# Mamba slots of a two-layer mixer: C products and u merged on GpSimd, neighbouring B products merged, the residual added by TensorE and copied by ScalarE, and the four engines' orders rewritten

## What is computed

```python
def _mamba_block(x, in_w, cw, cb, xp_w, dt_w, dt_b, A_log, D_skip, out_w):
    xm, z = jnp.split(jnp.einsum('bld,ed->ble', x, in_w), 2, axis=-1)
    ...                                   # causal convolution over 4 taps
    xm = jax.nn.silu(jnp.transpose(xc, (0, 2, 1)) + cb[None, None, :])
    dt, Bm, Cm = jnp.split(jnp.einsum('bld,ed->ble', xm, xp_w), [DT_RANK, DT_RANK + D_STATE], axis=-1)
    dt = jax.nn.softplus(jnp.einsum('blr,dr->bld', dt, dt_w) + dt_b)
    dA = jnp.exp(dt[..., None] * -jnp.exp(A_log))
    dBu = dt[..., None] * Bm[:, :, None, :] * xm[..., None]
    _, h = jax.lax.associative_scan(_scan_combine, (dA, dBu), axis=1)
    y = jnp.einsum('blds,bls->bld', h, Cm) + xm * D_skip
    return jnp.einsum('bld,od->blo', y * jax.nn.silu(z), out_w)

for i in range(N_LAYERS):
    x = x + _mamba_block(_layer_norm(x, ln_g, ln_b), ...)
```

## Time and profile before

| | us |
|---|---|
| median of 3 runs | 1511.6 (1506.72, 1511.6, 1511.95) |
| the profiled execution, its own time | 1509.6 |
| its span, first to last instruction | 1506.9 |
| PE busy in the span | 1297.4 (86%) |
| DVE busy | 1170.8 (78%) |
| POOL busy | 1129.8 (75%) |
| ACT busy | 1003.6 (67%) |

### The profile page before, as it was taken

One profiled execution on the slowest core, in us unless ns is written; L12 is line 12 of the kernel. 1 busy time (PEld: TensorE's weight loads), 2 busy tenths in 40 slices (PEclk: granted clock), 3 DMA queues, 4 the chain that ended last, 5 costly groups with the idle time before them and its releaser, 6 DMA issues.

```text
span 1506.9 us, 20348 instructions
## 1 busy us (share of the span) xinstructions
PE 1297.4 (86%) x5459; PEld 718.6 (48%) x5460; DVE 1170.8 (78%) x1739; ACT 1003.6 (67%) x2373; POOL 1129.8 (75%) x775
## 2 busy tenths in 40 slices
PE   5589988998999899989988899799489889888984
PEld 2233333333333333333433567799455556555653
DVE  7599999999999999999999866655344555455554
ACT  3587778777877887787778872333266666666673
POOL 6499999999999999999999950344456556554551
PEclk8799999999999999999999999899799999999996
DMA  4543363255335433642452514311200000000000
GB/s 162 226 169 127 154 244 152 102 202 210 127 130 231 169 138 142 243 162 103 191 225 114 181 61 140 98 49 47 67 14 8 13 16 22 12 10 9 8 9 7
DMA packets 49122, 169.33 MB, mean 112 GB/s; under 512 B 15720, under 2 KB 33580, under 8 KB 40860
## 3 DMA queue, kind: packets, MB, share of 16 engines
q1 hardware_dynamic: 46780, 163.84, 28.7%
q0 software_dynamic: 2272, 4.66, 1.3%
HBM read 160.81 MB, written 7.67 MB: 112 GB/s over the span
## 4 chain that ended last, share of the span: by engine, by line
PE 31%; DVE 25%; issue 16%; ACT 13%; POOL 13%; DMA 1%; DVEq 0%; POOLq 0%; ACTq 0%
DVE h L1226 12%; POOL h L1232 9%; DVE h L1205 6%; ACT banks L1189 6%; PE banks L399 5%; PE banks L723 3%; PE banks L782 3%; PE banks L761 2%; PE banks L408 2%; POOL h L1212 2%; PE banks L797 2%; PE banks L700 2%; PE banks L663 2%; PE banks L680 2%; ACT Cb L740 1%
## 5 line engine op out<-in xcount | busy, mean ns | idle before, releaser
L1232 POOL TENSOR_TENSOR h<-h,Cb 128x1024 f32<-128x1024 f32 x255 | 595.5, 2356 | 31.8 <-DVE h L1226 30.5
L1226 DVE TENSOR_TENSOR_SCAN h<-banks,h 128x1024 f32<-128x1024 f32 x256 | 575.7, 2279 | 16.3 <-ACT banks L1189 12.4
L1259 PE MATMUL banks<-h,ident 128*128 128x512 f32 x1024 | 481.3, 603 | 49.0 <-POOL h L1232 26.9
L1189 ACT ACTIVATE banks<-dt,A_cur 128x255 f32<-128x255 f32 x1024 | 424.8, 462 | 136.8 <-DVE h L1226 134.8
L1259 PEld LDWEIGHTS banks<-h,ident 128*128 128x128 f32 x1024 | 185.6, 190 | 310.3 <-issue 207.5
L1205 DVE TENSOR_TENSOR h<-Bb,banks 128x1024 f32<-128x1024 f32 x176 | 210.5, 1204 | 0.0
L1212 POOL TENSOR_TENSOR h<-Bb,u 128x1024 f32<-128x1024 f32 x80 | 189.0, 2363 | 0.6 <-POOL u L1158 0.6
L753 POOL TENSOR_SCALAR h<-h 128x128 f32<-128x128 f32 (+1 forms) x128 | 101.4, 807 | 106.5 <-DVE h L746 106.5
L753 POOL TENSOR_SCALAR Cb<-Cb,h 128x128 f32<-128x128 f32 (+1 forms) x128 | 96.0, 766 | 53.7 <-DVE h L746 53.6
L1087 PE MATMUL banks<-xn,wF 128*128 128x512 f32 x256 | 119.0, 609 | 10.2 <-ACT xn L1079 10.2
L770 DVE COPY Bb<-banks 128x384 f32<-128x384 f32 x64 | 35.5, 555 | 75.5 <-PE banks L761 72.7
(11 more groups left out here) (289 smaller groups left out, 2042.3 us busy)
## 6 DMA issues: line engine op xcount, KB each, us to landing
Bb<-scrX SPq DMA_DIRECT2D x32, 2048.0 KB, 7.1
Cb<-scrX SPq DMA_DIRECT2D x32, 2048.0 KB, 11.3
h<-in_L_ffn_w SPq DMA_DIRECT2D x2, 2048.0 KB, 8.4
by_expert<-Cb SPq DMA_DIRECT2D x39, 64.0 KB, 1.5
h<-in_conv_w SPq DMA_DIRECT2D x4, 512.0 KB, 3.9
scr<-h SPq DMA_DIRECT2D x3, 640.0 KB, 3.0
wF<-scr SPq DMA_DIRECT2D x3, 512.0 KB
dt<-in_pmask SPq DMA_DIRECT2D x4, 257.0 KB, 2.8
```

Source lines behind the costliest of these rows:

```text
L1189: m = e.activation(ps_dA[c % 2][:, g, half, 1:S], dts[q][:, half, i * S + 1:(i + 1) * S], ACT.Exp, scale=A_cur[q][:, s:s + 1])
L1226: e.tensor_tensor_scan(chunk(i, c), ps_dA_flat[c % 2], chunk(i, c), 0.0, ALU.mult, ALU.add).then_inc(sem("scan"), 1)
L1232: e.tensor_tensor(h[i][:, rows(c), :, :], h[i][:, rows(c), :, :], both(Cb[i], c), ALU.mult).then_inc(sem("hC"), 1)
L1259: m = e.matmul(bank(5), ident[:], h_flat[i][:, s * HALVES * S:(s + 1) * HALVES * S], start=(s == 0), stop=(s == NS - 1))
```

## The change

1. **POOL.** `pool_C` and `pool_mul` take several neighbouring chunks, and one instruction then covers them all; it raises its semaphore by the number of chunks when the last is done, and `pool_C` waits for the last chunk's scan. In slots 0 to 14 six pairs of C products become one instruction each (a0 a1, a2 a3, a5 a6, b0 b1, b3 b4, b5 b6). The two halves of u become one instruction of 128 x 1024.
2. **DVE.** The B products a1 a2, b1 b2 and b4 b5 become one instruction each, and DVE's products move ahead of the scans: in the new list no product stands directly before the scan of its own chunk.
3. **Residual.** `pe_out` adds one identity matmul over `xs` ahead of the two output matmuls, all into bank 5, so that PE adds the residual. ACT (`act_res`) copies bank 5 into `xs`; DVE no longer takes part, but for the very last pair.
4. **Orders.** All four lists of slots 0 to 14 are rewritten. The last slot keeps the unmerged order on POOL (`POOL_LAST`) and loses `res` on DVE, gains it on ACT.

The diff, cut where a list has only lines that stay as they are:

```diff
--- before.py
+++ after.py
@@ -1151,21 +1151,25 @@
             e.scalar_tensor_tensor(out=dts[q][:], in0=ps_dt, scalar=0.0, in1=sp[:], op0=ALU.max, op1=ALU.add
                                    ).then_inc(sem("dt"), 1)
 
-        def product_u(e, t, q, half):
+        def product_u(e, t, q, *half):
             e.wait_ge(sem("dt"), t + 1)
-            e.wait_ge(sem("xm"), 2 * t + half + 1)
+            e.wait_ge(sem("xm"), 2 * t + (half[0] + 1 if half else HALVES))
             wait(e, sem("ub"), 2 * t - 2)
-            e.tensor_tensor(us[q][:, half, :], dts[q][:, half, :], xm[q][:, half, :], ALU.mult
-                            ).then_inc(sem("u"), 1)
-        def rows(c):
-            return slice(GROUP * c, GROUP * c + GROUP)
-
-        def both(t, c):
-            return t[:, rows(c), :].unsqueeze(2).to_broadcast([P, GROUP, HALVES, S])
+            at = slice(half[0], half[0] + 1) if half else slice(0, HALVES)
+            e.tensor_tensor(us[q][:, at, :], dts[q][:, at, :], xm[q][:, at, :], ALU.mult
+                            ).then_inc(sem("u"), 1 if half else HALVES)
+        def rows(cs):
+            return slice(GROUP * cs[0], GROUP * cs[-1] + GROUP)
+
+        def both(t, cs):
+            return t[:, rows(cs), :].unsqueeze(2).to_broadcast([P, GROUP * len(cs), HALVES, S])
+
+        def u_rows(t, cs):
+            return t.unsqueeze(1).to_broadcast([P, GROUP * len(cs), HALVES, S])
 
         def act_ucopy(e, p, q, i):
             e.wait_ge(sem("u"), 2 * p + 2)
@@ -1198,20 +1202,18 @@
                 if i:
                     e.wait_ge(sem("scr"), 16 * (LAYERS - 1))
 
-        def dve_mul(e, p, q, i, c):
-            if c == DVE_MUL[i][0]:
+        def dve_mul(e, p, q, i, *cs):
+            if cs[0] == DVE_MUL[i][0]:
                 e.wait_ge(sem("ub"), 2 * p + i + 1)
             mul_ready(e, p, i)
-            e.tensor_tensor(h[i][:, rows(c), :, :], both(Bb[i], c),
-                            ps_u.unsqueeze(1).to_broadcast([P, GROUP, HALVES, S]), ALU.mult
-                            ).then_inc(sem("mulv"), 1)
-
-        def pool_mul(e, p, q, i, c):
+            e.tensor_tensor(h[i][:, rows(cs), :, :], both(Bb[i], cs), u_rows(ps_u, cs), ALU.mult
+                            ).then_inc(sem("mulv"), len(cs))
+
+        def pool_mul(e, p, q, i, *cs):
             e.wait_ge(sem("u"), 2 * p + 2)
             mul_ready(e, p, i)
-            e.tensor_tensor(h[i][:, rows(c), :, :], both(Bb[i], c),
-                            us[q][:, :, i * S:(i + 1) * S].unsqueeze(1).to_broadcast([P, GROUP, HALVES, S]), ALU.mult
-                            ).then_inc(sem("mulp"), 1)
+            e.tensor_tensor(h[i][:, rows(cs), :, :], both(Bb[i], cs), u_rows(us[q][:, :, i * S:(i + 1) * S], cs), ALU.mult
+                            ).then_inc(sem("mulp"), len(cs))
 
         def chunk(i, c):
             n = GROUP * HALVES * S
@@ -1226,16 +1228,16 @@
             e.tensor_tensor_scan(chunk(i, c), ps_dA_flat[c % 2], chunk(i, c), 0.0, ALU.mult, ALU.add
                                  ).then_inc(sem("scan"), 1)
 
-        def pool_C(e, p, q, i, c):
-            e.wait_ge(sem("scan"), CHUNKS * (2 * p + i) + c + 1)
+        def pool_C(e, p, q, i, *cs):
+            e.wait_ge(sem("scan"), CHUNKS * (2 * p + i) + cs[-1] + 1)
             e.wait_ge(sem(f"C{i}"), 16 * p + 16)
-            e.tensor_tensor(h[i][:, rows(c), :, :], h[i][:, rows(c), :, :], both(Cb[i], c), ALU.mult
-                            ).then_inc(sem("hC"), 1)
+            e.tensor_tensor(h[i][:, rows(cs), :, :], h[i][:, rows(cs), :, :], both(Cb[i], cs), ALU.mult
+                            ).then_inc(sem("hC"), len(cs))
 
         def dve_C(e, p, q, i, c):
             e.wait_ge(sem("scan"), CHUNKS * (2 * p + i) + c + 1)
             e.wait_ge(sem(f"C{i}"), 16 * p + 16)
-            e.tensor_tensor(h[i][:, rows(c), :, :], h[i][:, rows(c), :, :], both(Cb[i], c), ALU.mult
+            e.tensor_tensor(h[i][:, rows((c,)), :, :], h[i][:, rows((c,)), :, :], both(Cb[i], (c,)), ALU.mult
                             ).then_inc(sem("mulv"), 1)
 
         def pe_sum(e, p, q, i, c):
@@ -1268,15 +1270,21 @@
 
         def pe_out(e, p, q):
             e.wait_ge(sem("gate"), 2 * p + 2)
+            e.wait_ge(sem("res"), p + 1)
+            e.matmul(bank(5), ident[:], xs[:, cols(p)], start=True, stop=False)
             for half in range(HALVES):
                 m = e.matmul(bank(5), wS[:, SC_OUT + half * P:SC_OUT + (half + 1) * P],
-                             yz[:, half, :, :].rearrange("p i l -> p (i l)"), start=(half == 0), stop=(half == 1))
+                             yz[:, half, :, :].rearrange("p i l -> p (i l)"), start=False, stop=(half == 1))
             m.then_inc(sem("o_ps"), 1)
+
+        def act_res(e, p, q):
+            e.wait_ge(sem("o_ps"), p + 1)
+            e.activation(xs[:, cols(p)], bank(5), ACT.Copy).then_inc(sem("res"), 1)
 
         def dve_res(e, p, q):
             e.wait_ge(sem("o_ps"), p + 1)
             wait(e, sem("res"), p + NPAIR)
-            e.tensor_tensor(xs[:, cols(p)], xs[:, cols(p)], bank(5), ALU.add).then_inc(sem("res"), 1)
+            e.tensor_copy(xs[:, cols(p)], bank(5)).then_inc(sem("res"), 1)
 
 
 
@@ -1635,8 +1643,8 @@
                   dt=(1, pe_dt), sum=(0, pe_sum), out=(0, pe_out))
         ACTE = dict(square=(1, act_square), lnv=(1, act_lnv), rstd=(1, act_rstd), xn=(1, act_xn), xm=(1, act_xm),
                     zs=(1, act_zs), silus=(1, act_silus), exps=(1, act_exps), xd=(1, act_xd), sp_abs=(1, act_sp_abs), sp_exp=(1, act_sp_exp),
-                    sp_ln=(1, act_sp_ln), dA=(0, act_dA), ucopy=(0, act_ucopy))
-        DVE = dict(norm=(1, dve_norm), dt=(1, dve_dt), u=(1, product_u), mul=(0, dve_mul), scan=(0, dve_scan), gate=(0, dve_gate), res=(0, dve_res))
+                    sp_ln=(1, act_sp_ln), dA=(0, act_dA), ucopy=(0, act_ucopy), res=(0, act_res))
+        DVE = dict(norm=(1, dve_norm), dt=(1, dve_dt), u=(1, product_u), mul=(0, dve_mul), scan=(0, dve_scan), gate=(0, dve_gate))
         POOL = dict(u=(1, product_u), mul=(0, pool_mul), C=(0, pool_C))
 
         def in_order(table, order):
@@ -1727,7 +1735,7 @@
             e.tensor_tensor(center_g[:], center_w[:], center_g[:], ALU.mult).then_inc(sem("const"), 1)
             first(e, POOL, "u:0")
             slots(e, in_order(POOL, POOL_ORDER))
-            in_order(POOL, POOL_ORDER)(e, LAST, LQ, True, 0)
+            in_order(POOL, POOL_LAST)(e, LAST, LQ, True, 0)
             tail_gpsimd(e)
 
 
@@ -1907,17 +1915,16 @@
 
 
 PE_ORDER = """
-sum:l6 sum:l7 conv:0 out conv:1 sum:a0 sum:a1 sum:a2 z:0 z:1 sum:a3 sum:a4 sum:a5 xproj sum:a6 dt:0 dt:1 sum:a7
-sum:b0 +center sum:b1 +var sum:b2 sum:b3 sum:b4 sum:b5"""
+sum:l6 conv:0 conv:1 sum:l7 z:0 out z:1 sum:a0 sum:a1 sum:a2 xproj sum:a3 dt:0 dt:1 sum:a4 sum:a5 sum:a6 sum:a7
++center +var sum:b0 sum:b1 sum:b2 sum:b3 sum:b4 sum:b5"""
 ACT_ORDER = """
-xn dA:a2 dA:a3 dA:a4 silus xm:0 xm:1 exps dA:a5 ucopy:b dA:a6 dA:a7 dA:b0 silus zs:0 zs:1 exps dA:b1 xd dA:b2
-sp_abs sp_exp sp_ln dA:b3 dA:b4 +square dA:b5 +lnv +rstd dA:b6 ucopy:n dA:b7 dA:n0 dA:n1"""
+xn dA:a2 dA:a3 dA:a4 silus xm:0 xm:1 exps dA:a5 ucopy:b dA:a6 res dA:a7 dA:b0 silus zs:0 zs:1 exps dA:b1 xd dA:b2
+sp_abs dA:b3 sp_exp sp_ln dA:b4 dA:b5 +square dA:b6 +lnv ucopy:n dA:b7 dA:n0 +rstd dA:n1"""
 DVE_ORDER = """
-norm mul:a0 scan:a0 mul:a1 scan:a1 gate:l mul:a2 scan:a2 res mul:a4 scan:a3 scan:a4 mul:a6 scan:a5 scan:a6 scan:a7
-mul:b0 scan:b0 mul:b1 mul:b2 scan:b1 mul:b4 scan:b2 gate:a dt mul:b5 scan:b3 scan:b4 mul:b7 scan:b5 scan:b6 scan:b7"""
+mul:a0 mul:a12 norm scan:a0 scan:a1 scan:a2 mul:a4 scan:a3 scan:a4 mul:a6 gate:l scan:a5 scan:a6 mul:b0 mul:b12
+scan:a7 scan:b0 mul:b45 scan:b1 scan:b2 scan:b3 mul:b7 dt scan:b4 gate:a scan:b5 scan:b6 scan:b7"""
 POOL_ORDER = """
-C:l7 mul:a3 C:a0 mul:a5 C:a1 mul:a7 C:a2 C:a3 C:a4 C:a5 C:a6 C:a7 mul:b3 C:b0 mul:b6 C:b1 C:b2 u:0 u:1 C:b3
-C:b4 C:b5 C:b6"""
+mul:a3 C:l7 mul:a5 C:a01 C:a23 mul:a7 mul:b3 mul:b6 C:a4 C:a56 C:a7 C:b01 C:b2 u C:b34 C:b56"""
...
@@ -1926,13 +1933,15 @@
 ACT_LAST = """
-sq:0 rs:0 sc:0 dA:a2 id:0 dA:a3 sq:1 rs:1 sc:1 dA:a4 id:1 dA:a5 ucopy:b sq:2 dA:a6 rs:2 sc:2 dA:a7 id:2 dA:b0 dA:b1
+sq:0 rs:0 sc:0 dA:a2 id:0 dA:a3 sq:1 rs:1 sc:1 dA:a4 res id:1 dA:a5 ucopy:b sq:2 dA:a6 rs:2 sc:2 dA:a7 id:2 dA:b0 dA:b1
...
 DVE_LAST = """
-mul:a0 scan:a0 mul:a1 scan:a1 gate:l mul:a2 scan:a2 res mul:a4 scan:a3 scan:a4 mul:a6 scan:a5 scan:a6 scan:a7
+mul:a0 scan:a0 mul:a1 scan:a1 gate:l mul:a2 scan:a2 mul:a4 scan:a3 scan:a4 mul:a6 scan:a5 scan:a6 scan:a7
 mul:b0 scan:b0 mul:b1 mul:b2 scan:b1 mul:b4 scan:b2 gate:a scan:b3 mul:b5 scan:b4 mul:b7 scan:b5 scan:b6 scan:b7"""
+POOL_LAST = """
+C:l7 mul:a3 C:a0 mul:a5 C:a1 mul:a7 C:a2 C:a3 C:a4 C:a5 C:a6 C:a7 mul:b3 C:b0 mul:b6 C:b1 C:b2 C:b3 C:b4 C:b5 C:b6"""

```

## The result

The changed kernel took **1527.8 us** (median of 4 runs, 1524.9 to 1530.4) beside 1510.8 for the kernel before (4 runs, 1506.7 to 1512.0): a ratio of 1.0117, interval 1.0088 to 1.0146. It is slower by 17 us, where 1489 had been forecast. The profiled execution took 1529.65 with a span of 1527.7, 20.8 more than before.

A forecast was written before the change was run, and what follows sets the result against it. The prediction took DVE and POOL, both full, to bound the slots together. Savings of 14 x 1.15 + 3.9 + 1.0 = 21.0 us, against a known average of 1510.0, gave 1489 us, range 1482 to 1501.

The forecast's parts named there:

- the one on PE: PE, slots 1 to 14: two more records, 0.94 us; last sum behind the convolution; slack 2.5 to 3.6, cost nothing.
- rival 2: PE's last sum is late by 3.7 us more, so DVE waits 1.15 at gate:l; 1505 us; chance 0.08.
- Rival 3: TensorE falls to its lower clock behind the last sum of a, eight records a slot; 1520 us; chance 0.05.
- The last slot: Last slot: DVE loses 2.05 us of work and waiting, POOL enters 2 us late; bounds 0 and 2.05, 1.0 saved.
- Behind the slots: Stages after the slots: not touched, so they only shift, with no change in length.
- DVE: DVE, slots 1 to 14: residual 0.58, moved products 0.48 and merges 0.09 save 1.15 us a slot, leaving 50.53.
- the four moved products: DVE products a0, a1, a2, b0 no longer directly before their own scans: 0.12 us each, 0.48 a slot.
- POOL: POOL, slots 1 to 14: seven merges save 0.82 us a slot, bounds 0 and 0.82, leaving 50.39 of work.
- Rival 1: POOL's merges save nothing because cost goes by elements; only the old 0.47 wait is won; 1498.5 us; chance 0.15.
- ACT: ACT, slots 1 to 14: gains a 0.60 us copy, to 41.4 of 50.5; slack 2.7 and about 0.2, cost nothing.
- Slot 0: First slot: DVE's products move into its idle time ahead of norm, saving 3.9 us.
- SP: SP's queue: C of a released some 6 us later, B earlier; the queue has room, cost nothing.

The follow-up runs named there:

- skip_sem: Changed kernel with sequence b's skip matmuls put ahead of the convolution under their own semaphore, which xm awaits instead of y; 1491.2 us.
- last_slot_early: skip_sem with, in slot 14 alone, gate:a ahead of the scan of b4 and the C products of b5 and b6 as two instructions; 1490.3 us.
- residual_dve: skip_sem with the residual added by DVE again, without the identity matmul and without ACT's copy; 1506.4 us.
- gate_a_early: Changed kernel with gate:a ahead of scan b4, b's first sums ahead of center and var, and some ACT work later; 1522.2 us.
- pool_unmerged: skip_sem with every C product and both halves of u as single instructions on POOL again, same order; 1495.7 us.

## Why the prediction was wrong

**The step that failed** is the one on PE: "so y at 15.8 and gate:l due at 19.4 ... Slack 2.5 to 3.6, cost nothing". It asked when the sum's *result* is needed, and not who else waits for the semaphore `y`. xm does, and it was due at 15.8 from the end of the scan of b6: that scan ends at 428.41 - 3.31 - 2.18 = 422.9 (norm, less three products' worth and one scan), and the table is loaded at 438.7. By the prediction's own number for y the slack was zero. skip_sem shows that this wait is the cause.

**The same walk was short by one sum.** It counted "b5 b6 done at 4.6, then ... one sum 1.7". Both sums wait for the merged product. Measured from 422.9: product done at 4.7, two sums 3.6, convolution 6.9, skip and last sum 2.7, so y at 18.0. The 2.2 between 15.8 and 18.0 is xm's wait. gate:l itself was never late; rival 2 had PE's late sum, but at gate:l, and from 3.7 us of lateness on; xm felt 2.2.

**Rival 3 came in part, at its named place.** The clock falls behind the last sum of a, around center and var, but in some slots only and for a few records, 1.25 us a slot and about 5 us of the 17.8 (four slots). The rival asked for eight slow records in every slot. Its argument against, "a wait of 1.86 leaves the clock at 1.00", did not carry over to two shorter waits with two matmuls between them. The Trainium skill (TensorE: Matmul & The Clock Gate, Part 1) says that an idle array falls back to half its clock. The trace agrees where it fell, 1.12 us to 2.07 for the same records, and in the slot after, with the same waits, it did not fall.

**The last slot** was forecast at -1.0 and took +3.8. Its gate:l still stands at its old, early place, behind the scan of a1, and waits 4.87 us for y. I had let POOL's delay of 2 us count and not PE's: in slot 14 the sums of b stand behind gate:a, center and var. With gate:a earlier and b5, b6 apart, last_slot_early has 2.2 less of this wait.

**Behind the slots** I forecast a plain shift ("The stages behind the slots are not touched"); it is +3.4. One step of that was wrong by itself: the last pair's out is done behind the last gate, and it has the new identity matmul too. Its output matmuls (L1276) start 926.86 - 925.15 = 1.71 after the gate, and 908.49 - 907.74 = 0.75 before; what PE does behind them is 0.86 later up to 28 us behind the gate. It is so in every variant but residual_dve, which lacks that matmul and is 0.00 later. Another 0.8 comes at PE's eight routing matmuls, before and then after:

```profile
936.19 1.04 PE L1450 MATMUL banks<-Bb 128*128 128x8 f32 x8
954.46 1.83 PE L1458 MATMUL banks<-Bb 128*128 128x8 f32 x8
```

The clock falls 29.4 us behind the last gate in both profiles (at 937.1 and 954.5), but then the eight were all but done, and now they have only begun. PE's second token transpose, which waits for its gather, starts 957.65 - 907.74 = 49.9 after the last gate before, and 977.01 - 925.15 = 51.9 after it now: +1.95, of which 1.65 was there when the gather was issued (950.74 and 969.80). The other 1.4 come later and stay open.

**What held**, measured with xm's wait out of the way (skip_sem):

- DVE: the slot went from 51.69 to 50.40 with the same 0.17 of waiting ahead of a5, so 1.29 saved where 1.15 was forecast. The residual alone is 0.60 (0.58 forecast, residual_dve). A merged pair costs 440.98 - 438.80 = 2.18 against 2.24, so three merges save 0.18 (0.09). The rest, 0.51, fits what the four moved products were to save (0.48); it is left over by subtraction, and no run moved them back alone. The Trainium skill (VectorE: DVE Perf Modes, Rules for kernel authors) would have this last at nothing, and by the other two rows the whole at 0.78; the measured 1.29 speaks against it.
- POOL: 0.74 for the merges, 0.82 forecast. Rival 1 (nothing) falls.
- ACT: its copy of the residual waits up to 1.1 for PE and delays no scan (DVE waits for dA 1.7 us in all from 200 to 800, as before). Slot 0: 4.1 for 3.9 (norm at 110.46 before, mul:a0 at 106.32 in skip_sem). SP: no wait of POOL or DVE for B or C shows among the slots' waits.
- The slot itself: 50.53 forecast, 50.40 with skip_sem, and the whole 1491.2 against 1489. This is another kernel than the one that the forecast was for, which took 1527.8.

## What to carry to other kernels

When work moves behind other work on a queue, list every `wait` on the semaphore that it raises, buffer releases included, and give each waiter its own due time; the consumer of the result is often not the first. A semaphore that stands for several events (the sum is complete, and the xm buffer is free) ties them together: splitting it cost no matmul and gave 36.6 us. When products are merged, count everything that stood behind the *first* of them, because it now waits for the last. And a matmul added to a loop is added to its last pass too, where nothing may hide it.

## What the hardware did that I had not expected

- The granted clock fell in a few slots out of fourteen that show the same instructions and the same waits (1.16 and 0.69 us around two matmuls). Those of the changed kernel lie in windows in which the DMA share is near 1, but so do those at 310 and 415 us in which it stayed at 1.00; and in residual_dve it fell at a DMA share of 0.00 (435 to 440 us, 0.66). So the transfers do not decide it. No run tells what does.
- Filling those gaps (gate_a_early) removed all dips between 90 and 900 us, and was worth 0.25 us a slot by itself.
- Behind the slots the granted clock falls at different places in different executions, and with it the time: from 1150 to 1270 us it is 0.94 in skip_sem and 1.00 in pool_unmerged.
- With DVE and POOL both over 99% busy and PE at 94% (skip_sem, 390 to 490 us), no slowing of POOL by DVE shows. A B product on POOL is 2.34 us long at 51.18, where DVE stands idle, and 2.35 at 448.92, where DVE is full.
